# Attention, output projection and quantised feed-forward of one sequence per core: how the softmax sums of the last head are formed and how its outputs are scaled

## What is computed

```python
q, k, v = (proj(wq), proj(wk), proj(wv))
q, k = apply_rope(q, k, sin, cos)
att = jnp.einsum('bhqd,bhkd->bhqk', q, k) * (1.0 / math.sqrt(HD))
att = jax.nn.softmax(att, axis=-1)
y = jnp.einsum('bhqk,bhkd->bhqd', att, v)
return y.transpose(0, 2, 1, 3).reshape(b, t, c) @ wo.T
...
x = _layernorm(x + _L0_attn_ref(x, wq, wk, wv, wo))
x = _layernorm(x + _L0_ffn_ref(x, ...))      # down(silu(gate(x)) * up(x)), W = (wq - 128) * scale
```

## Time and profile before

| | us |
|---|---|
| median of 3 runs (lowest) | 3202.3 (3201.14) |
| the profiled execution | 3208.55 |
| its span, slowest core (core 3) | 3207.0 |
| spans of the other cores | 3200.5 to 3205.9 |
| busy: TensorE, VectorE, ScalarE | 3170.4, 1474.1, 842.2 |
| first score matmul, first matmul of the output projection (core 3) | 78.59, 1150.87 |

### The profile page before, as it was taken

How to read it: one execution, slowest core, us unless ns; L and a number is a source line. 1 busy time by engine, 2 the same in 40 slices (tenths; PEclk the granted TensorE clock), 3 DMA queues, 4 the chain that set the end, 5 groups by cost and what they waited for, 6 DMA issues and landing times.

```text
span 3207.0 us, 40569 instructions; the slowest of 8 cores (3200.5 to 3207.0 us)
## 1 busy us (share of the span) xinstructions
PE 3170.4 (99%) x14624; PEld 1431.6 (45%) x14624; DVE 1474.1 (46%) x1917; ACT 842.2 (26%) x924; POOL 192.4 (6%) x348
## 2 busy tenths in 40 slices
PE   7999999999999999999999999999999999999998
PEld 3444444444444444444444444444444444444444
DVE  1888888899988843321111111233322211111334
ACT  0555555555556633310000000000000000000002
POOL 1000000000000000000010000000000001100000
PEclk9999999999999999999999999999999999999999
DMA  9454445533434569964434645677456646533555
GB/s 150 79 72 69 69 67 67 71 56 63 64 60 66 76 144 259 264 166 79 76 72 76 105 79 95 133 148 156 108 103 153 142 92 105 90 68 61 103 102 168
DMA packets 213283, 335.01 MB, mean 104 GB/s; under 512 B 122208, under 2 KB 138080, under 8 KB 206816
## 3 DMA queue, kind: packets, MB, share of 16 engines
q0 software_dynamic: 49536, 180.38, 33.9%
q1 hardware_dynamic: 163408, 151.51, 21.1%
q10 hardware_dynamic: 144, 0.52, 0.0%
HBM read 433.40 MB, written 54.39 MB: 152 GB/s over the span
## 4 chain that ended last, share of the span: by engine, by line
PE 98%; DMA 1%; ACT 0%; issue 0%; DVE 0%; POOL 0%; ACTq 0%; DVEq 0%; SPq 0%; POOLq 0%
PE PS L696 19%; PE PS L689 19%; PE PS L683 19%; PE PS L590 19%; PE PS L661 7%; PE PS L609 7%; PE PS L639 7%; PE PS L575 1%; DMA AB<-wk_c 1%; DMA AB<-AB 0%; ACT AB L740 0%; PE PS L627 0%; DVE AB L879 0%; POOL AB L494 0%; POOL AB L489 0%
## 5 line engine op out<-in xcount | busy, mean ns | idle before, releaser
L590 PE MATMUL PS<-AB 128*128 128x512 bf16 x2816 | 691.8, 380 | 0.0
L740 ACT ACTIVATE AB<-PS 128x1024 bf16<-128x1024 f32 x512 | 524.0, 1024 | 419.3 <-PE PS L609 390.2
L689 PE MATMUL PS<-AB 128*128 128x512 bf16 x2816 | 622.1, 379 | 0.0
L683 PE MATMUL PS<-AB 128*128 128x512 bf16 x2816 | 622.1, 379 | 0.0
L696 PE MATMUL PS<-AB 128*128 128x512 bf16 x2816 | 608.1, 379 | 0.0
L939 DVE SCALAR_TENSOR_TENSOR AB<-PS,AB 128x1024 bf16<-128x1024 f32 x88 | 113.0, 1284 | 952.2 <-PE PS L689 952.2
L879 DVE TENSOR_TENSOR AB<-AB 128x1024 f32<-128x1024 f32 x372 | 454.4, 1222 | 67.0 <-ACT AB L740 52.1
L793 ACT ACTIVATE AB<-PS,AB 128x1024 f32<-128x1024 f32 x88 | 98.1, 1114 | 1389.9 <-PE PS L683 1389.9
L590 PEld LDWEIGHTS PS<-AB 128*128 128x128 bf16 x2816 | 276.3, 98 | 334.7 <-issue 10.2
L689 PEld LDWEIGHTS PS<-AB 128*128 128x128 bf16 x2816 | 275.7, 98 | 332.1
L696 PEld LDWEIGHTS PS<-AB 128*128 128x128 bf16 x2816 | 275.5, 98 | 332.2
(11 more groups left out here) (58 smaller groups left out, 1205.5 us busy)
## 6 DMA issues: line engine op xcount, KB each, us to landing
AB<-wg_c POOLq DMA_DIRECT2D x88, 512.0 KB, 6.4
AB<-wu_c POOLq DMA_DIRECT2D x88, 512.0 KB, 8.4
AB<-wd_c POOLq DMA_DIRECT2D x88, 512.0 KB, 6.4
AB<-rl_sp SPq DMA_DIRECT2D x64, 256.0 KB, 5.8
AB<-x SPq DMA_DIRECT2D x16, 1024.0 KB, 7.3
x1f<-AB SPq DMA_DIRECT2D x16, 1024.0 KB, 9.6
AB<-x1f SPq DMA_DIRECT2D x64, 256.0 KB, 7.8
AB<-wk_c POOLq DMA_DIRECT2D x16, 512.0 KB, 7.1
```

Source lines behind the costliest of these rows:

```text
L590: mm = t.matmul(bank(6 + n % 2)[:, 0:512], W[wi % NW][:, di * 128:(di + 1) * 128], x_block(di, c), start=(di == 0), stop=(di == NDI - 1))
L683: mm = t.matmul(bank(par * 4 + c)[:, 0:512], GW[i % 3][:, di * 128:(di + 1) * 128], X1T_V[:, 4 * c:4 * c + 4, di], start=(di == 0), stop=( ...
L689: mm = t.matmul(bank(par * 4 + 2 + c)[:, 0:512], UW[i % 3][:, di * 128:(di + 1) * 128], X1T_V[:, 4 * c:4 * c + 4, di], start=(di == 0), st ...
L740: sc.activation(P[u % NP], bank(2 * (u % 2), 2)[:, 0:1024], AF.Exp, bias=-C_SHIFT, scale=ASCL).then_inc(act_exp, 1)
```

## The change

1. Last head (groups 60 to 63, m >= LAST = 60): VectorE adds units 0, 2, 4 and 6 only (3 adds) and closes; TensorE sums units 1, 3, 5 and 7 with the matrix of ones two slots after each unit (`unit_sums`), and adds the closed half with one more matmul in slot 4 of the next group (`group_sums`). The sums then stand in all 128 partitions of a PSUM bank; VectorE takes their reciprocal there (128x512) straight into RB and multiplies. The DMAs L340, L346, L350, L357 and the row copies of ScalarE are gone for these groups, and all products are made before the output tiles.
2. The closing add reads and writes in plain order; the store to rl_sp takes over the reordering (`"(j p) -> p j"`, single elements of 4 bytes).
3. For groups 0 to 59 the reduction stands 16 slots and the product 25 slots after the group's first slot, the DMAs between move with them.
4. `filled`: projections from slot 1 on; the last 32 matmuls in slots 480 to 483 and 485 to 488 (4 each). The last job uses the bank of the one before it.
5. K of head 1, second half: copied by VectorE, no longer by ScalarE.
6. wo row 11, and so 12 to 15 behind it, waits until the last RB (of group 59) has landed. The load of y (L368) moves from slot 500 to 494, the loads of x from 504 to 503.

```diff
-SUM_PE = NM - 2
+LAST = NM - 4
...
     def filled(s):
         if s <= 480:
-            return max(0, s - 3) * (16 * NJ - 40) // 477
-        return 16 * NJ - 40 + min(40, 4 * min(s - 480, 2) + 2 * max(0, s - 482))
+            return max(0, s - 1) * (16 * NJ - 32) // 479
+        return 16 * NJ - 32 + min(16, 4 * (s - 480)) + min(16, 4 * max(0, s - 485))
+    def job_bank(n):
+        return bank(6 + (n % 2 if n < NJ - 1 else (NJ - 2) % 2))
...
     def l_bank(m):
-        return bank(6 + m % 2)
+        return bank(7 - m % 2)
+    def acc_done(m):
+        return 8 * m if m <= LAST else 8 * LAST + 4 * (m - LAST)
...
-                m = (s - 14) // 8
-                if k == 6 and SUM_PE <= m < NM:
-                    s_.wait_ge(act_l, m - SUM_PE + 1)
-                    s_.wait_ge(dve_r, m - 1)
-                    s_.dma_start(out=LQ[m % 2], in_=LROW[m % 2]).then_inc(lq_ld[m % 2], 16)
-                m = (s - 21) // 8
-                if k == 5 and 0 <= m < NM:
+                m = (s - 17) // 8
+                if k == 1 and 0 <= m < LAST:
                     s_.wait_ge(dve_r, m + 1)
-                    s_.dma_start(out=rl_sp[m].rearrange("(p j) -> p j", j=4),
-                                 in_=RLQ[m % 2]).then_inc(rl_st[m % 2], 16)
+                    s_.dma_start(out=rl_sp[m].rearrange("(j p) -> p j", p=128),
+                                 in_=RLQ[m % 2], allow_slow_non_contiguous=True).then_inc(rl_st[m % 2], 16)
...
             for y in range(8, NH):
+                if y == 11:
+                    g.wait_ge(rb_ld[(LAST - 1) % 2], 16 * (LAST // 2))
...
+            def unit_sums(s):
+                m, k = divmod(s, 8)
+                if k == 1:
+                    if m < LAST + 2:
+                        t.wait_ge(act_job, NJ - 2 + 2 * (m - LAST))
+                    else:
+                        t.wait_ge(dve_r, m - 1)
+                t.wait_ge(act_exp, s + 1)
+                for kk in range(2):
+                    mm = t.matmul(l_bank(m)[:, 0:512], ONB, P[s % NP][:, kk * 512:(kk + 1) * 512],
+                                  start=(k == 1 and kk == 0), stop=False)
+                mm.then_inc(pe_ps, 1)
+
+            def group_sums(m):
+                t.wait_ge(dve_acc, acc_done(m + 1))
+                t.matmul(l_bank(m)[:, 0:512], ONB, ACCB[m % 2], start=False, stop=True).then_inc(pe_l, 1)
...
+                if s >= 8 * LAST + 3 and k % 2 == 1:
+                    unit_sums(s - 2)
+                if k == 4 and m > LAST:
+                    group_sums(m - 1)
                 t.wait_ge(act_exp, s + 1)
-                if m >= SUM_PE:
-                    if k == 0:
-                        t.wait_ge(act_job, NJ - 1 + m - SUM_PE)
-                    for kk in range(2):
-                        mm = t.matmul(l_bank(m)[:, 0:512], ONB, P[s % NP][:, kk * 512:(kk + 1) * 512],
-                                      start=(k == 0 and kk == 0), stop=(k == 7 and kk == 1))
-                    if k == 7:
-                        mm.then_inc(pe_l, 1)
...
+            unit_sums(NU - 1)
+            group_sums(NM - 1)
...
                 else:
-                    v.wait_ge(lq_ld[m % 2], 16)
-                if m >= 2:
-                    v.wait_ge(rl_st[m % 2], 16 * (m // 2))
-                v.reciprocal(RLQ[m % 2], LQ[m % 2]).then_inc(dve_r, 1)
+                    v.wait_ge(pe_l, m - LAST + 1)
+                    v.wait_ge(dve_y, m - 1)
+                    v.reciprocal(RB[m % 2], l_bank(m)[:, 0:512]).then_inc(dve_r, 1)
...
-                        v.tensor_tensor(ACCB[m % 2].rearrange("p (j q) -> p q j", j=4),
-                                        ACC[m % 2][:, 0:512].rearrange("p (q j) -> p q j", j=4),
-                                        ACC[m % 2][:, 512:1024].rearrange("p (q j) -> p q j", j=4),
+                        v.tensor_tensor(ACCB[m % 2], ACC[m % 2][:, 0:512], ACC[m % 2][:, 512:1024],
                                         AL.add).then_inc(dve_acc, 1)
...
-                if k == 4 and 20 <= s < 20 + 8 * NM:
-                    recip((s - 20) // 8)
-                if k == 5 and 29 <= s < 29 + 8 * (NM - 2):
-                    y_scale((s - 29) // 8)
+                if k == 0 and 16 <= s < 16 + 8 * LAST:
+                    recip((s - 16) // 8)
+                if k == 1 and 25 <= s < 25 + 8 * LAST:
+                    y_scale((s - 25) // 8)
+                if k == 5 and s >= 13 + 8 * LAST:
+                    recip((s - 13) // 8)
+                if k == 2 and s >= 18 + 8 * LAST:
+                    y_scale((s - 18) // 8)
```

More of the change, by code:

```diff
@@ L48 @@
 OFF_ACCB = 184 * KB
-OFF_LROW = 186 * KB
+OFF_LT = 186 * KB
 OFF_RB = 190 * KB
@@ L149, in build_program @@
     ACCB = [bf16(OFF_ACCB + i * 1024, 128, 512) for i in range(2)]
-    LT = [bf16(OFF_LROW + i * 2048, 128, 512) for i in range(2)]
-    LROW = [f32(OFF_LROW + i * 2048, 1, 512) for i in range(2)]
+    LT = [bf16(OFF_LT + i * 1024, 128, 512) for i in range(2)]
     LQ = [f32(OFF_LQ + i * 16, 128, 4) for i in range(2)]
@@ L335, in _ @@
                 m = (s - 10) // 8
-                if k == 2 and 0 <= m < SUM_PE:
-                    s_.wait_ge(dve_acc, 8 * (m + 1))
+                if k == 2 and 0 <= m < LAST:
+                    s_.wait_ge(dve_acc, acc_done(m + 1))
                     if m >= 2:
@@ L358, in _ @@
                                  in_=rl_sp[m:m + 1, :].to_broadcast([128, 512])).then_inc(rb_ld[m % 2], 16)
-                m = (s - 30) // 8
-                if k == 6 and 0 <= m < 60:
+                m = (s - 28) // 8
+                if k == 4 and 0 <= m < LAST:
                     s_.wait_ge(dve_y, m + 1)
@@ L586, in job_matmul @@
                     if n < 2:
-                        t.wait_ge(act_pro, 4)
+                        t.wait_ge(dve_pro, 5)
+                    elif n == NJ - 1:
+                        t.wait_ge(act_job, n)
                     else:
                         t.wait_ge(act_job, n - 1)
-                mm = t.matmul(bank(6 + n % 2)[:, 0:512], W[wi % NW][:, di * 128:(di + 1) * 128],
+                mm = t.matmul(job_bank(n)[:, 0:512], W[wi % NW][:, di * 128:(di + 1) * 128],
                               x_block(di, c),
@@ L729, in _ @@
                 sc.copy(VTS[:, hf * 1024:(hf + 1) * 1024], bank(2, 2)[:, 0:1024]).then_inc(act_pro, 1)
-                sc.wait_ge(pe_pro, 4 * hf + 4)
-                sc.copy(KT[1][:, hf * 1024:(hf + 1) * 1024], bank(6, 2)[:, 0:1024]).then_inc(act_pro, 1)
+                if hf == 0:
+                    sc.wait_ge(pe_pro, 4)
+                    sc.copy(KT[1][:, 0:1024], bank(6, 2)[:, 0:1024]).then_inc(act_pro, 1)
             def expo(u):
@@ L760, in _ @@
                     y_out(m - 1)
-                if k == 5 and m > SUM_PE:
-                    sums_row(m - 1)
                 for n in range(filled(s) // 16, filled(s + 1) // 16):
@@ L864, in y_scale @@
                 v.tensor_tensor(dst, YU[m % 3], RB[m % 2], AL.mult).then_inc(dve_y, 1)
-            for s in range(NU + 30):
+            for s in range(NU + 11):
                 m, k = divmod(s, 8)
                 if s < NU:
-                    if m >= SUM_PE:
-                        pass
+                    if m >= LAST:
+                        if k == 2:
+                            v.wait_ge(act_exp, s + 1)
+                            v.wait_ge(dve_acc, acc_done(m - 1))
+                            v.tensor_tensor(ACC[m % 2], P[(s - 2) % NP], P[s % NP], AL.add).then_inc(dve_acc, 1)
+                        elif k in (4, 6):
+                            v.wait_ge(act_exp, s + 1)
+                            v.wait_ge(dve_acc, acc_done(m) + k // 2 - 1)
+                            v.tensor_tensor(ACC[m % 2], ACC[m % 2], P[s % NP], AL.add).then_inc(dve_acc, 1)
                     elif k == 1:
```

58 lines of the change are left out of this document (34 added, 24 removed).

## The result

The changed kernel takes 3656.8 us (median; lowest 3651.4), the kernel before 3202.3: ratio 1.141, 95% interval 1.139 to 1.143. (Medians and lowest times are over all executions of a kernel; every ratio compares only those in which neither half of the chip ran longer at a lower clock.) The forecast was 3198.0. The slowest core's span grew from 3207.0 to 3649.9 us.

A forecast was written before the change was run, and what follows sets the result against it. TensorE, busy for 99% of the span, was taken as the bound. Start -0.9, eight moved matmuls +1.7 and last head -5.1 sum to -4.3 us: 3202.3 - 4.3 = 3198.0 us, range 3190 to 3203.5.

The forecast's parts named there:

- Groups 0 to 59: Closing add, 4-byte store and shorter lags before the last head: VectorE freed 1.75 us per group, TensorE gains nothing, price 0.
- the slots' slack of 13 us: Groups 0 to 59: six slots of room between the spread's issue and the product, likewise for a transpose.
- Start of the slots: First slots: wait of 1.52 us becomes 1.10, second wait of 0.51 filled by projections in slot 1; gain 0.9 us.
- The first stretch: First scores to scores of slot 480: 1021.1 us before, 0.9 off at its start, 1.7 added by eight projection matmuls.
- Last head: Slots 480 to 511: 16.3 + 28.3 + 0.5 = 45.1 us against 51.2, plus 1.0 for low clock, giving -5.1.
- the 44 to 47 named as the sign: Last head: a length of 44 to 47 us would show the forecast right, one of 50 us wrong.
- the ring: Slots 489 to 511, TensorE and ScalarE waiting on each other in turn: 1.23 us per slot instead of 1.44, 28.3 us.
- The reciprocal: Last head, 512 columns wide on VectorE: 2.1 us estimated from 3.7 ns per column, bounds 0.7 and 4.8.
- Rival (b): Last head: long reciprocal delays adds, deciding from 2.4 us in the last group, 4.8 in every group; 3202.0 us, chance 0.10.
- wo gate: Before the output projection: last wo load lands between 1152 and 1156, cost 0, with 2 to 6 us of margin.
- Rival (c): Output projection: late wo loads stall TensorE, by 19.5 us if they land one after another; 3217.5 us, chance 0.09.
- Closing addition: End of each group on VectorE, in plain order: near 0.7 us instead of 2441 ns.

The follow-up runs named there:

- Run 4: The kernel of run 3 plus, per group, a second store of the same 512 values in packed 4-byte pieces, waited for only two groups later: ratio 1.163.
- run 5: As Run 4, but each 4-byte piece of the second store lies 64 bytes from the next in device memory: ratio 0.9985.
- run 1: The changed kernel with the old 16-byte store and reordering closing addition put back for groups 0 to 59: 3200.6 us, ratio 0.9992.
- Run 15: The kernel of run 1 with the reciprocal of group 62 moved behind the closing addition of group 63 on VectorE: 3197.9 us, ratio 0.9976.
- run 3: The changed kernel with the old 16-byte store, the plain closing addition kept, and the reordering done in the product: ratio 1.0014.
- run 13: As the second kernel of runs 4 and 8, but each full 64-byte stretch is filled from four neighbouring partitions: lowest 3593.4 us, 1.12 by lowest times.
- runs 4 and 8: Run 4, and the same with its second store as 32 full 64-byte stretches 1 KB apart, in four transfers: the latter 3800.8 us, ratio 1.182.
- Run 12: The kernel of run 3 plus an unwaited second store: 64 runs of eight packed 4-byte pieces, one per 64 bytes, in four transfers: ratio 1.013.
- run 10: The kernel of run 3 plus an unwaited second store of 512 4-byte pieces 8 bytes apart, eight in every 64 bytes: ratio 0.9994.

## Why the prediction was wrong, point by point

**The step that failed** is "Groups 0 to 59", the store with single 4-byte elements: "1 us more", bounded by 11 us, on the ground that "2 KB are latency and no bandwidth", and that "even several us more reach nobody". It cost some 450 us. Two errors sit in it. The size: SyncE waits 16 us on the mean for the store before it issues the spread, 24.3 at most, in the group shown 19.8 us from issue to issue, where I bounded the landing at 3.7 + 11. The kind, which matters more: I asked only who waits for this transfer, and never what it does to the others. Run 4 shows that nobody need wait for it. In the changed kernel the spread went from 5.8 to 9.8 us, wk from 7.1 to 18.4, the transposes from 4.7 to 6.2, and between the late store and these the slots' slack of 13 us was spent. The prediction counted only "four times the pieces"; run 5 has more of them at no cost. Four 16-byte pieces share each 64 bytes in the old store, sixteen 4-byte ones in the new.

The Trainium skill has two sentences near this. Page "DMA: Bandwidth & Descriptors", section "Specifications", says that below 512 bytes a DMA engine does a read-modify-write. By that alone old and new stores are alike, and so are runs 4 and 5, which differ by 0.16 in the ratio; the rule does not tell them apart. The section "Back-pressure in remote DMA" of that page says, of another kind of transfer, that stalled writes stall the other queues of their engine too. The landings here look like that, since GpSimd's loads are late too, but no run shows what happens inside.

**Start of the slots.** Right. Forecast: projections in slot 1 and one wait of 1.10. The changed kernel:

```profile
80.15 0.59 PE L656 MATMUL PS<-AB 128*128 128x512 bf16 x2 [1.04 <-DVE AB L855]
80.58 0.59 PE L613 MATMUL PS<-AB 128*128 128x512 bf16 x2
81.01 1.24 PE L594 MATMUL PS<-AB 128*128 128x512 bf16 x5
```

The wait is 1.04 us, and the 0.51 of the earlier trace rows is gone. The profile puts the wait down to VectorE's copy of K, but the program lets this product wait for the first exp and not for that copy (L652 waits for the four copies before it), and the product starts as long behind the end of the exp as before (some 0.36 us).

The first stretch, to the scores of slot 480, took 1017.0 us in run 1 against my 1021.1 - 0.9 + 1.7 = 1021.9. Its granted clock is 1.00, where I had let the low stretches like the earlier trace rows stay. That fits the 5 us that I put down to them, and the gain is luck: nothing in the sum gave it.

**Last head.** Too low by 2 us: 48.0 us in run 1, forecast 46.1 (45.1 and 1.0 for the clock), and above the 44 to 47 named as the sign. The waits for V's transpose and the rotary embedding are gone, as forecast. Slots 480 to 488 took 16.0 (16.3), and the ring 1.24 per slot (1.23), from 1111.43 to 1137.48 for 21 slots. The miss is the end: it was given 0.5 us and took some 3.5, 1.78 for the closing addition, 0.58 for y, the rest partly at a low clock. On the other seven cores, which don't wait for y, the head took 47.1 to 47.2. The output projection starts at 1143.42 (forecast some 1146) only because the first stretch was shorter.

**The reciprocal** was mis-sized: forecast 2.1 us, measured 3.35.

```profile
L874 DVE RECIPROCAL AB<-PS 128x512 f32<-128x512 f32 x4 | 13.4, 3351 | 0.0
```

That is 6.5 ns per column; the slope of 3.7 ns had come from rows of 1 and 8 columns. Rival (b) was right on where it decides, from 2.4 us on: the matmul that closes the head waits behind it (1.78 us), and nothing else does. Run 15 takes this wait away and gains it. The estimate of 4.3 us by the page "VectorE: DVE Perf Modes" in the Trainium skill was too long by 0.95 us, mine too short by 1.25.

**wo gate.** Right: no wait for wo. In run 1 the gate opens at 1117.67, 9 us before my 1126.5 (5 of them are the shorter first stretch). The five loads are issued from there to 1120.1, the slowest lands 23.6 us after its issue, by 1143.7 (forecast 1152 to 1156), before row 15 is needed. Rival (c) didn't come. **Closing addition:** 0.69 us as forecast.

**The sum without the failed step** is run 1: 0.9992, some 2.5 us less than before, where -4.3 was forecast; the interval, -6 to +1 us, holds the forecast and zero. In the profiled executions the two stretches took 1064.9 us against 1072.3 on the slowest cores, 7.4 less: 4.1 in the first, where I had 0.8 more, and 3.2 in the last head, where I had 5.1 less. The two errors have opposite signs. (The ratio shows less than 7.4 because the median before lies under its profiled execution.) The chance of 0.98 for "same" stood on bounds of one transfer's latency, which left the effect on its neighbours out.

## What to carry to other kernels

Before a store to device memory is cut into smaller pieces, ask how many pieces fall into each 64 bytes, and not only how many there are or who waits: 4 cost no time here, 8 made the other transfers slower (wk 10.4 to 12.9 us instead of 7.1) and cost 1.3% at most, 16 cost a seventh of the run time. An order that is needed anyway is cheaper on a compute engine with room (0.4 us in the product, run 3). Spreading the pieces out was free too, though only for the second store (run 5). And a duration that is extrapolated from 8 columns to 512 is a guess: put nothing behind such an instruction that the critical engine waits for.

## What the runs showed of the hardware

- Sixteen 4-byte writes into each 64-byte stretch of device memory, 32 such stretches every 25 us or so per core on eight cores, slow the core's other DMA: the loads of wk (512 KB) from 7.1 us to 16.9 in run 13, 18.4 in the changed kernel, 22.3 and 25.2 in runs 4 and 8, at a lower total rate (49 GB/s against 69). The same number of 4-byte writes with a stretch each does not (8.8 us). Whether one core alone would show it wasn't tried, and packed writes into on-chip memory neither. Run 12 against run 10 says that packing within 32 bytes matters too.
- In the waiting stretch of the changed kernel the granted clock is 0.88 on the mean. The waits of TensorE sum to some 320 of the 443 us, so the rest is short gaps and matmuls at a low clock.
- A wait of 1.78 and one of 0.58 us, close together, were followed by 8 us at a granted clock of 0.57 on one core (run 1), and 1.78 and 0.61 us on another by none (run 3). What the clock goes by is open.
